# A four-layer graph network on one core: layers 2 and 3 apply the attention to x before the projection, one graph per half of the array

## What is computed

```python
Wh = jnp.einsum('bnd,de->bne', x, W)
e_src = jnp.einsum('bnd,d->bn', Wh, a_src)
e_dst = jnp.einsum('bnd,d->bn', Wh, a_dst)
logits = e_src[:, :, None] + e_dst[:, None, :]
logits = jnp.where(logits >= 0, logits, NEG_SLOPE * logits)
logits = jnp.where((adj == 0)[None], -jnp.inf, logits)
attn = jax.nn.softmax(logits, axis=-1)
out = jnp.einsum('bnm,bmd->bnd', attn, Wh)
x = _layernorm(x + out)
```

## Time and profile before

| what | value |
|---|---|
| median of 3 runs | 3392.47 us (3390.36 to 3393.5) |
| span of the profiled execution | 3390.5 us |
| own time of the profiled execution | not listed apart from its span; the lowest run is 3390.36 us |
| TensorE busy over the span | 97% |
| VectorE, GpSimd, ScalarE busy | 64%, 59%, 50% |
| granted TensorE clock, mean | 0.992 of full |
| last block | from about 2320 us to the end |
| one step of the last block | 16.05 us |

### The profile page before, as it was taken

One profiled execution on the slowest core, in us unless ns is written; L12 is line 12 of the kernel. 1 busy time (PEld: TensorE's weight loads), 2 busy tenths in 40 slices (PEclk: granted clock), 3 DMA queues, 4 the chain that ended last, 5 costly groups with the idle time before them and its releaser, 6 DMA issues. The chain is left out here.

```text
span 3390.5 us, 58748 instructions
## 1 busy us (share of the span) xinstructions
PE 3273.9 (97%) x16217; PEld 2651.5 (78%) x16217; DVE 2186.4 (64%) x4753; ACT 1691.7 (50%) x4193; POOL 1989.9 (59%) x2870
## 2 busy tenths in 40 slices
PE   8999989999999999999999999996999999999997
PEld 6777768888888888888888888885777777777775
DVE  6777655555555555555555555555778877877775
ACT  2111135555555555555555555543665666666665
POOL 4555564444444444444444444433888888888886
PEclk9999999999999999999999999998999999999999
DMA  4343310000000000000000000002111111111110
GB/s 140 118 127 126 94 47 16 19 19 19 19 19 19 19 19 19 19 19 19 19 19 19 19 19 19 19 25 90 41 47 56 46 46 56 46 46 50 52 46 28
DMA packets 76527, 143.98 MB, mean 42 GB/s; under 512 B 8640, under 2 KB 8640, under 8 KB 76480
## 3 DMA queue, kind: packets, MB, share of 16 engines
q1 hardware_dynamic: 73920, 135.07, 12.1%
q0 software_dynamic: 2560, 8.39, 0.9%
HBM read 93.09 MB, written 50.33 MB: 42 GB/s over the span
## 5 line engine op out<-in xcount | busy, mean ns | idle before, releaser
L715 POOL TENSOR_TENSOR w_first<-xin,v_row 128x512 f32<-128x512 f32 x512 | 719.9, 1427 | 493.6 <-ACT w_first L753 482.8
L845 DVE TENSOR_TENSOR hT_lo<-hv,hT_hi 128x512 fp32r<-128x512 f32 x256 | 296.7, 1159 | 428.8 <-ACT hT_hi L771 428.8
L47 PE MATMUL whp<-big_hi,xT_hi 128*128 128x512 f32 x1024 | 422.6, 413 | 0.0
L47 PE MATMUL wop<-big_hi,hT_hi 128*128 128x512 f32 x1024 | 405.2, 396 | 0.0
L47 PE MATMUL wop<-big_hi,hT_lo 128*128 128x512 f32 x1024 | 401.0, 392 | 0.0
L47 PE MATMUL whp<-big_lo,xT_hi 128*128 128x512 f32 x1024 | 401.0, 392 | 0.0
L47 PE MATMUL whp<-big_hi,xT_lo 128*128 128x512 f32 x1024 | 400.6, 391 | 0.0
L47 PE MATMUL wop<-big_lo,hT_hi 128*128 128x512 f32 x1024 | 398.7, 389 | 0.0
L767 ACT COPY wh<-whp 128x512 f32<-128x512 f32 x256 | 149.0, 582 | 384.3 <-PE whp L47 384.3
L1139 POOL TENSOR_TENSOR g_terms<-x,g_v_row 128x512 f32<-128x512 f32 x256 | 329.0, 1296 | 5.0 <-ACT x L1219 4.9
L753 ACT ACTIVATE w_first<-w_first 128x512 f32<-128x512 f32 x512 | 319.4, 627 | 5.1 <-POOL w_first L715 5.1
(11 more groups left out here) (200 smaller groups left out, 8018.8 us busy)
## 6 DMA issues: line engine op xcount, KB each, us to landing
xt<-in_x SPq DMA_DIRECT2D x64, 256.0 KB, 2.7
x_scratch<-x SPq DMA_DIRECT2D x64, 256.0 KB, 2.0
xin<-x_scratch SPq DMA_DIRECT2D x64, 256.0 KB, 2.6
att_scratch<-attT SPq DMA_DIRECT2D x64, 256.0 KB, 2.0
att<-att_scratch SPq DMA_DIRECT2D x64, 256.0 KB, 2.7
x1r<-x_scratch SPq DMA_DIRECT2D x64, 256.0 KB, 3.0
out<-res SPq DMA_DIRECT2D x64, 256.0 KB, 2.0
stage<-in_L_gnn_W_heads POOLq DMA_DIRECT2D x16, 256.0 KB, 2.9
```

Source lines behind the costliest of these rows:

```text
L47: ins = nc.tensor.matmul(out, a, b, start=first and c == 0 and q == 0, stop=last and c == n - 1 and q == 2)
L715: nc.gpsimd.tensor_tensor(terms[:, k % TR, :], xin[:], v_row[:, k, :], ALU.mult).then_inc(terms_ready, 1)
L845: nc.vector.tensor_tensor(hT[h % 2][1][:].rearrange("p c n -> p (c n)"), hv[h % 2][:], hT[h % 2][0][:].bitcast(F32).rearrange("p c n -> p ...
```

## The change

`Attention` gets a flag `compact`: the two 64 by 64 blocks of the turned attention are put at columns 0 to 63 of their own rows instead of on the diagonal of a 128 by 128 matrix. PSUM banks `bank_a`, `turn_2`, `turn_3` and `smallq` go; two banks `agg_banks` and two small ones for the scores come. In layers 2 and 3 `turn_x`, `x_hi`, `x_lo`, `wh_out` and `sums` go. `aggregate` comes: eight fp32 matmuls per tile, each with 64 rows of x by 128 columns as weights and 64 columns of attention moving; graph 0 works in array rows 0 to 63 and writes one bank, graph 1 in rows 64 to 127 and writes the other. Its result is the transposed attn x. ScalarE copies it as hi halves in two copies of 256 columns a row (`agg_hi`), VectorE makes the lo halves in two (`agg_lo`), and `project` now multiplies that by W and leaves the result in `g.sums`, where `residual` reads it.

The new parts, and what leaves TensorE's program:

```diff
-                def turn_x(g, t, x, ready):
-                    pe.wait_ge(ready, t + 1)
-                    ge(pe, g.xT_lo_ready, t)
+                def aggregate(g, t, x, other, count):
+                    pe.wait_ge(g.att.turned_ready, 2 * t + 2)
+                    ge(pe, other.agg_lo_ready, 2 * count)
                     for c in range(KC):
-                        ins = nc.tensor.transpose(g.turn[:, c, :], x[:, c * P:(c + 1) * P], ident[:])
-                    ins.then_inc(g.xT_done, 1)
+                        for k in range(2):
+                            own = slice(k * NODES, (k + 1) * NODES)
+                            ins = nc.tensor.matmul(agg[:, k, c, :], x[own, c * P:(c + 1) * P],
+                                                   g.att.turned[own, 0, 0:NODES], start=True, stop=True)
+                    ins.then_inc(g.agg_done, 1)
 
                 def project(g, t):
-                    pe.wait_ge(g.xT_lo_ready, t + 1)
+                    pe.wait_ge(g.agg_lo_ready, 2 * t + 2)
+                    ge(pe, g.z_ready, t)
...
-                    product(nc, bank_a[:], g.xT, (w_hi, w_lo),
-                            [(c, g.q + c) for c in range(KC)]).then_inc(g.wh_done, 1)
+                    product(nc, g.sums[:], g.aggS, (w_hi, w_lo),
+                            [(c, g.q + c) for c in range(KC)]).then_inc(g.sums_done, 1)
...
                 def step(n, r):
+                    if live(n, 3):
+                        project(g2, n - 3)
                     if live(n, 4):
-                        if live(n, 3):
-                            pe.wait_ge(g2.att.turned_ready, 2 * (n - 2))
                         g3.att.pe_turn(nc, pe, n - 4, ident)
                     if live(n, 2):
-                        ge(pe, g3.wh_ready, n - 3)
-                        project(g2, n - 2)
...
                         spread(g2, n - 2)
...
-                    if live(n, 3):
-                        turn_x(g3, n - 3, x3[(r - 3) % 2], g2.x_ready)
                     if live(n, 4):
-                        sums(g3, n - 4)
+                        aggregate(g3, n - 4, x3[r % 2], g2, capped(n - 2, T))
...
-                    if live(n, 1):
-                        turn_x(g2, n - 1, x2[(r - 1) % R], x2_ready)
-                    if live(n, 3):
-                        ge(pe, g2.wh_ready, capped(n - 1, T))
-                        project(g3, n - 3)
...
-                        spread(g3, n - 3)
+                    if live(n, 4):
+                        project(g3, n - 4)
...
+                    if live(n, 3):
+                        spread(g3, n - 3)
                     if live(n, 2):
-                        sums(g2, n - 2)
+                        aggregate(g2, n - 2, x2[(r - 2) % R], g3, n - 3)
```

ScalarE's and VectorE's new helpers:

```diff
+                def agg_hi(g, t):
+                    act.wait_ge(g.agg_done, t + 1)
                     ge(act, g.sums_done, t)
+                    for k in range(2):
+                        nc.scalar.copy(by_graph(g.aggS[0][:])[:, k], agg[:, k]).then_inc(g.agg_hi_ready, 1)
...
+                def agg_lo(g, t):
+                    for k in range(2):
+                        dve.wait_ge(g.agg_hi_ready, 2 * t + k + 1)
+                        nc.vector.tensor_tensor(by_graph(g.aggS[1][:])[:, k], agg[:, k],
+                                                by_graph(g.aggS[0][:].bitcast(F32))[:, k], ALU.subtract
+                                                ).then_inc(g.agg_lo_ready, 1)
```

More of the change, by code:

```diff
@@ L1050, in __init__, with by_graph @@
                         sem(name + "_terms_ready"))
-            g2 = Gat("g2", 2 * KC, 0, turn_2)
-            g3 = Gat("g3", 3 * KC, 2 * P, turn_3)
+            g2 = Gat("g2", 2 * KC, small_2)
+            g3 = Gat("g3", 3 * KC, small_3)
+            def by_graph(tile):
+                return tile.rearrange("p c (g n) -> p g c n", g=2)
             weights = (w1, w2, W2, W3)
@@ L1244, in step @@
                         dots(g3, n - 3)
-                    if live(n, 1):
-                        x_hi(g2, n - 1)
-                    if live(n, 3):
-                        wh_out(g3, n - 3)
+                    if live(n, 2):
+                        turned(g2, n - 2)
+                    if live(n, 4):
+                        ge(act, res_stored, 16 * (n - 4))
+                        normalise(g3.norm, n - 4, g3.z[:], res[:], g3.x_ready)
                     if live(n, 3):
@@ L1251, in step @@
                     if live(n, 2):
-                        turned(g2, n - 2)
+                        agg_hi(g2, n - 2)
                     if live(n, 1):
                         dots(g2, n - 1)
-                    if live(n, 4):
-                        ge(act, res_stored, 16 * (n - 4))
-                        normalise(g3.norm, n - 4, g3.z[:], res[:], g3.x_ready)
                 def weights_hi(k):
@@ L1381, in step @@
                         nc.vector.tensor_tensor(h1[:], bank_b[:], b1_row[:], ALU.add).then_inc(h1_ready, 1)
-                    if live(n, 3):
-                        x_lo(g3, n - 3)
                     if live(n, 4):
-                        residual(g3, n - 4, x3[r % 2][:])
+                        agg_lo(g3, n - 4)
                     if live(n, 0):
@@ L1400, in step @@
                         peak(g3, n - 3)
+                    if live(n, 2):
+                        agg_lo(g2, n - 2)
+                    if live(n, 3):
                         g3.att.dve_after_exp(nc, dve, n - 3, gate)
@@ L1424, in spread @@
+                    product(nc, g.sums[:], g.aggS, (w_hi, w_lo),
+                            [(c, g.q + c) for c in range(KC)]).then_inc(g.sums_done, 1)
                 def spread(g, t):
                     pe.wait_ge(g.att.diag_ready, t + 1)
+                    ge(pe, g.att.turned_ready, 2 * t)
                     nc.tensor.matmul(g.att.scores_psum, same_graph[:], g.att.diag[:, 0, :],
                                      start=True, stop=True).then_inc(g.att.scores_done, 1)
[L1429 to L1436, removed]
```

75 lines of the change are left out of this document (26 added, 49 removed).

## The result

The changed kernel takes 3905.53 us (median of 4 runs, 3904.11 to 3907.52) beside 3392.98 us before: 1.151 times as long, with an interval of 1.1494 to 1.1527. That is 513 us more. The forecast was 377 more, and its range ended at 3860: the sign and most of the mechanism came true, the size did not.

A forecast was written before the change was run, and what follows sets the result against it. TensorE's work was taken to bound the kernel, with VectorE's chain to h1 just behind. 3390.5 + 291 (longer steps) + 12 (last steps) + 73 (clock) = 3767, or 3769 us against the runs' median; range 3655 to 3860.

The forecast's parts named there:

- The ring: Last block: TensorE and VectorE wait for each other in turn; step 20.82 us instead of 16.05, +291 us over 61 steps.
- Item 1: VectorE's residual of g2 to h1, then h1, lo halves of g3 and hand-over: projection of g3 starts at 8.91 us.
- the optional term: VectorE's gate product might start before GpSimd's long products and take less than 1.06 us: -0.6 us a step.
- Item 2: TensorE: g3's projection 2.83 us, then the second product with g2's turn inside 2.99 us; together 5.82.
- Item 3: From `spread(g3)` through exponential and copies to g2's lo halves: 3.05 us, with the aggregate hidden.
- Item 4: TensorE: 12 matmuls of g2's projection, the last landing after 0.39 us instead of 0.23: 3.04 us.
- The clock: TensorE's clock falls after some 4 us idle, slowing g3's projection: 1.2 us a step, 73 us in 61 steps.
- the clock falls twice: Rival: the wait before g2's projection costs clock too, 1.6 + 1.0 us a step, 3855 us; chance 0.16.
- The tail: Last four steps: the last tile passes aggregate, copies and projection twice, and step 64's residual is late: +12 us.
- The halves: TensorE's aggregate: the two half-array matmul streams overlap, 16 instructions in 0.9 us; 1.65 if one after another.
- Faster: Rival: VectorE's residual isn't late, g2's lo halves ready under 0.5 us after the aggregate; 3312 us, chance 0.04.
- What was to be seen: Signs: step near 22 us, VectorE idle 3 to 5 us before g2's residual, clock well below 1.00, aggregates about 0.9 us.

The follow-up runs named there:

- with the clock held up: Changed kernel plus unread matmuls, 14 after the aggregate of g3 and 11 after that of g2, filling both waits of a step: 3716.09 us, ratio 1.0947.
- With the other wait filled: Changed kernel plus 14 unread matmuls in the wait before the transposes of h1 alone: 3779.74 us, ratio 1.1134.
- the last kernel: Reordered attention-first kernel with full-row aggregate, against the 3446.03 us one: `dots(g3)` and `project(g2)` split in two; 3444.36 us, ratio 1.0151.
- The two kernels at 3446.03 and 3447.25 us: Attention first with all four engines reordered, differing only in the aggregate: full rows 3446.03 us, ratio 1.0156; halves 3447.25 us, ratio 1.0158.

## Why the prediction was partly right

**The ring (right in kind; the exact sum is luck).** The sum of 20.82 us a step is the 20.8 measured with the clock held up. The steady steps and what leads into them cost 296 us against a forecast of 291. But its parts erred in both directions by half a microsecond, and that they cancel is luck. Item 1 was 8.41 us, not 8.91, for two opposite reasons. The chain up to h1 took 6.28 us (2991.74 to 2998.02) instead of 7.44, mostly by the optional term: the gate product took 0.16 us (2997.95), not 1.06. From h1 to the projection it took 2.13 instead of 1.47, because VectorE waited 0.62 us for ScalarE's hi copies of g3 (2999.34), and ScalarE had first to do the norm of tile n-1 (2998.10). The forecast had the aggregate of g3 off the ring and left out that its copies queue there. Item 2 was 5.75 at full clock (2.87 and 2.88), against 5.82. Item 3 was 3.45, not 3.05, and not through the copies, which at 375 and 419 ns came out by the values taken: one small operation of the scores took 0.74 us beside GpSimd's long one (3008.18) and held up the exponential. With the clock held up it was 3.56. Item 4 was put at 3.04; it was 3.10 with the clock held up and 4.65 without, and this is the clock.

**The clock (the step that failed).** The prediction said: "I take 1.2 us a step", once a step, in the projection of g3. Measured against the run with both waits filled are 1.58 us there (4.45 less 2.87) and 1.55 in g2's projection (4.65 less 3.10), 3.1 us a step, and 190 us in all instead of 73. The first part was shaved below its own upper end of 1.6, though the low stretch lay almost wholly in the projection. The second was the rival "the clock falls twice", with a chance of 0.16: it was the right mechanism at too low a price, 1.0 us, on the thought that a shorter wait costs less. In the changed kernel it does not: 2.08 us idle cost as much as 2.54. (With the other wait filled, the 2.1 us cost it in three steps of four.) With 1.6 twice the working would have given 3392.5 + 303 + 195 = 3891.

**The tail (right in kind, half the size).** The forecast gave the last steps 12 us. With the clock held up they cost 24, with the clock's fall 29. The four exit steps run the same ring with less beside it; which of their waits makes the other 12 was not tried.

**The halves.** The 16 instructions of an aggregate take 1.04 us (2990.95 to 2991.99); 0.9 was taken and 1.65 was the bound. The Trainium skill (TensorE: Matmul & The Clock Gate, Part 3) says that loads and matmuls of different row groups overlap, and the trace agrees: the two halves of a chunk start 0.007 us apart (2995.126 and 2995.132), and from the second pair on a pair starts every 0.112 us. Full-row ones start every 0.112 us too, so a pair costs what the one full-row instruction does that it replaces. The rest of the 0.19 us by which an aggregate of halves is dearer lies at its two ends. From the last matmul of a product to the first of the aggregate are 0.32 us with halves and 0.23 with full rows, and from its last matmul to the next instruction 0.20 and 0.11. Full rows, in the last kernel:

```profile
2932.00 1.11 PE L1406 MATMUL agg_banks<-g_turned,x 128*128 128x128 f32 x8
2932.95 0.33 PE L1424 MATMUL small<-g_diag,same_graph 128*128 128x64 f32 x2
```

The Trainium skill (TensorEngine Tiling, Key Properties) says that a change of the tiling mode drains TensorE. The traces fit that, at about 0.09 us a switch instead of the 0.16 bounded ahead. In the changed kernel it falls into the waits behind the aggregates and costs nothing. The two kernels at 3446.03 and 3447.25 us can't put a price on it: with halves, TensorE's wait for h1 shrank from 23.0 to 16.3 us (2500 to 3300 us), and the runs came out 1.2 us apart.

**The rival on the other side.** "Faster" asked for g2's lo halves within 0.5 us of the aggregate's end. The change has 2.1 us of waiting there. Ten kernels with other orders or other aggregates were tried; in the last one that wait is 0.4 us at most, and it still ended 1.5% above the kernel before.

**What was to be seen.** VectorE idle for 3.8 us ahead of the residual, TensorE idle for 2.54 us ahead of h1's transposes (3 to 4 forecast) and 2.08 ahead of g2's projection (1 to 2): as foretold in place. The aggregates took 1.04 us, not 0.9. The step was 23.9 and not 22.

## What to carry to other kernels

A wait of TensorE ahead of dense work can cost twice: once as idle time, and once as the clock of the work behind it. Here waits of 2.1 and 2.5 us ahead of twelve 512-column matmuls each cost another 1.6 us in every step of the changed kernel, and the 2.1 us wait alone in three steps of four. Where two operations that were beside one another come to depend on one another (aggregate, copy, project), the pipeline needs a place between them on every engine, not on TensorE alone; saving 0.7 us of matmuls a step is nothing against one open copy of 2 us. A few matmuls that nobody reads, in the wait, show within one run how much of a loss is the clock, as long as they end before the wait does.

## What the runs showed that was not expected

- More matmuls, less time: 1600 idle ones took the changed kernel from 3905 to 3716 us.
- The clock of TensorE stayed full during the idle time and fell in the work behind it, in each step of the changed kernel at the same two places, with the second product at full clock between the two.
- Full rows and halves came out within 1.2 us of each other at 3446 us, with TensorE busy for 95% of the stretch from 2500 to 3300 us: even then its own work did not set the step.
- Two halves of the array worked side by side at no extra cost for each pair; what the halves cost more was the way in and out of that mode, 0.09 us each.
- Two small operations of VectorE, the slope and the gate product, take three to six times as long when they fall beside a long one of GpSimd: 0.21 and 0.74 us for the slope in one step (2996.51 and 3008.18), and 0.16 against 1.06 for the gate product. Others beside the same long operation, such as the scores at 3007.86 (0.28 us, as elsewhere), do not.
